# Fourth logits copied ahead of the tags; additions and statistics of batch b+2 woven into batch b's latents; expert weights loaded in halves

## The reference, cut to what matters

```python
x = x + attn_a(layernorm(x), w_in, w_out)          # 16 heads, causal
x = x + ffn(layernorm(x), gate_w, w1, b1, ...)     # L = 0
x = x + attn_b(layernorm(x), Wqa, Wqb, Wkva, ...)  # latents, rotary part, 16 heads
x = x + ffn(layernorm(x), gate_w, w1, b1, ...)     # L = 1, same weights

def ffn(x):
    logits = xf @ gate_w                      # 2048 x 8
    top_logits, top_idx = top_k(logits, 2)
    gates = softmax(top_logits)
    routed = sum over the two experts of gate * (gelu(xf @ w1[e] + b1[e]) @ w2[e] + b2[e])
    shared = gelu(xf @ shared_w1 + shared_b1) @ shared_w2 + shared_b2
    return routed + shared

q_latent = h @ Wqa                            # 512 -> 384
kv_comp = h @ Wkva                            # 512 -> 128 + 64, rotary on the 64
```

## Time and profile before

| | |
|---|---|
| median of three runs | 2495.82 us (2493.22 to 2500.20) |
| profiled execution, its own time | 2501.03 us |
| its span, first to last instruction | 2499.2 us |
| mean granted TensorE clock | 0.975 of full |
| TensorE busy | 94% |
| VectorE / ScalarE / GpSimd busy | 65% / 46% / 26% |

### The profile page before, as it was taken

The page is one execution under the profiler, slowest core; times in us unless marked ns, Lnnn a source line. Parts: engine busy times, 40 slices in busy tenths (PEclk is TensorE's granted clock), DMA queues, the critical chain, the costliest instruction groups (busy, mean ns, idle before and its releaser), DMA issues. The chain is left out here.

```text
span 2499.2 us, 41690 instructions
## 1 busy us (share of the span) xinstructions
PE 2359.7 (94%) x13140; PEld 2015.4 (81%) x13140; DVE 1630.5 (65%) x3774; ACT 1143.1 (46%) x2698; POOL 657.7 (26%) x546
## 2 busy tenths in 40 slices
PE   6999999999999999988998779999999999879997
PEld 5888888989898989767877568888888888657885
DVE  6555555555555555674545748988888888865446
ACT  4444444344444443442333336666666666532334
POOL 1111111111111010043221224444443434253223
PEclk9999999999999999989999989999999999899998
DMA  4424243333423335117664100000000000136765
GB/s 164 177 91 175 92 155 110 132 133 115 147 106 138 127 117 200 51 72 262 243 230 161 47 10 10 18 9 18 9 18 9 18 9 9 34 110 229 254 211 227
DMA packets 100852, 277.65 MB, mean 111 GB/s; under 512 B 8641, under 2 KB 9081, under 8 KB 95121
## 3 DMA queue, kind: packets, MB, share of 16 engines
q1 hardware_dynamic: 79888, 220.77, 24.9%
q0 software_dynamic: 11360, 37.76, 3.9%
q10 hardware_dynamic: 9504, 17.85, 2.3%
HBM read 131.34 MB, written 145.00 MB: 111 GB/s over the span
## 5 line engine op out<-in xcount | busy, mean ns | idle before, releaser
L609 DVE SCALAR_TENSOR_TENSOR x<-bank,inv,x 128x512 f32<-128x512 f32 x512 | 361.6, 744 | 173.2 <-PE bank L76 170.9
L619 DVE TENSOR_TENSOR hq_lo<-bank,hq_hi 128x512 fp32r<-128x512 f32 (+1 forms) x320 | 201.2, 637 | 272.6 <-ACT hq_hi L531 104.2
L74 PE MATMUL bank<-xT_hi,w_hi 128*128 128x512 f32 x864 | 351.2, 407 | 18.0 <-POOL w_lo L700 7.3
L497 ACT ACTIVATE s<-s,top 128x128 f32<-128x128 f32 (+3 forms) x512 | 282.1, 553 | 155.7 <-DVE top L601 155.7
L76 PE MATMUL bank<-xT_hi,w_lo 128*128 128x512 f32 x864 | 344.7, 399 | 0.0
L75 PE MATMUL bank<-xT_lo,w_hi 128*128 128x512 f32 x864 | 344.5, 399 | 0.0
L563 ACT ACTIVATE hq_hi<-bank 128x512 fp32r<-128x512 f32 x128 | 76.5, 597 | 388.2 <-PE bank L76 388.2
L74 PE MATMUL bank<-wo_hi,hq_hi 128*128 128x512 f32 (+1 forms) x576 | 233.6, 406 | 1.0 <-DVE xT_lo L178 0.7
L75 PE MATMUL bank<-wo_lo,hq_hi 128*128 128x512 f32 (+1 forms) x576 | 228.4, 396 | 0.3 <-issue 0.3
L76 PE MATMUL bank<-wo_hi,hq_lo 128*128 128x512 f32 (+1 forms) x576 | 227.8, 395 | 0.2 <-issue 0.2
L601 DVE CUSTOM_DVE_ANT_0 s<-bank,mask 128x128 f32<-128x128 f32 (+3 forms) x512 | 216.7, 479 | 4.3 <-PE bank L76 4.3
(11 more groups left out here) (285 smaller groups left out, 5859.3 us busy)
## 6 DMA issues: line engine op xcount, KB each, us to landing
sorted_x<-blank SPq DMA_DIRECT2D x48, 1584.0 KB, 10.9
arena<-split_w SPq DMA_DIRECT2D x16, 2048.0 KB
split_w<-arena SPq DMA_DIRECT2D x48, 512.0 KB, 3.0
raw<-dram_wr SPq DMA_DIRECT2D x24, 512.0 KB, 5.7
w_raw<-dram_wa SPq DMA_DIRECT2D x16, 512.0 KB, 3.7
arrived<-routed_y SPq DMA_DIRECT2D x8, 1024.0 KB, 7.9
row_pt_hi<-sorted_x ACTq DMA_DIRECT2D x22, 264.0 KB
row_pt_lo<-sorted_x ACTq DMA_DIRECT2D x20, 264.0 KB
```

What stands on the lines that cost most here:

```text
L74: nc.tensor.matmul(out, hi, mov_hi, start=first, stop=False)
L497: nc.scalar.activation(at, at, ACT.Exp, bias=m.top[:, b, t:t + 1], scale=-1.0, accum_out=m.rowsum[:, b, t:t + 1]).then_inc(a.probs_ready, 1)
L609: nc.vector.scalar_tensor_tensor(out=xt, in0=m.bank[6 + t % 2][:, :], scalar=m.inv[:, b, t:t + 1], in1=xt, op0=ALU.mult, op1=ALU.add).then ...
L619: return nc.vector.tensor_tensor(out, bank, hi.bitcast(F32), ALU.subtract).then_inc(done, 1)
```

## The change

In the gate, ScalarE's order of `tag(1)` and `logits(3)` is swapped, and TensorE waits for the chain's read before it turns the fourth logits into the same bank. Behind the tiles, scaling of batch 1 moves behind the transposes of batch 0 and that of batch 2 up into the FFN, that of batch 3 into latents 0; GpSimd's sum of batch 2 moves up too; the last `down` and its additions are split among the transposes of the next norm. In the latents, additions, statistics and start of a batch move one batch ahead: batch 1's stay at (0, OPEN); batch b + 2's additions stand behind tile 0, its statistics behind tile 1 of batch b, its start behind the subtractions. The up half of an expert's weights is loaded once its slot's last up product is done, the down half after the last down product, the bias after the last output.

```diff
-def latent_scalar(nc, act, m, l, rt, first, then):
+def latent_scalar(nc, act, m, l, rt, first, scale, then):
     for b in range(B):
         for i in range(OPEN, NT - 1):
...
         nc.scalar.activation(m.ctok[:, b, :], m.bank[7][:, :], ACT.Copy).then_inc(l.tok_out, 1)
         act.wait_ge(l.rope_added, b + 1)
         nc.scalar.activation(m.xT[HI][HALF:P, b, KQ, :], m.qf[HALF:P, :], ACT.Copy).then_inc(l.rope_hi, 1)
-
-
-def latent_vector(nc, dve, m, l, first):
+        if b == 0:
+            scale()
+
+
+def latent_vector(nc, dve, m, l, first, begin):
...
+        if b + 2 < B:
+            begin(b + 2)
         if b < B - 1:
             rotary(b)
 
...
 def latent_gpsimd(nc, pool, m, l, a, sum_up, then, combined):
     for b in range(B):
-        if b + 2 < B:
-            if b:
-                pool.wait_ge(l.rope_lo, b)
-            sum_up(b + 2)
+        if b == 1:
+            pool.wait_ge(l.rope_lo, b)
+            sum_up(B - 1)
         if b == B - 1:
             pool.wait_ge(l.rope_lo, b)
             then()
 
     def turn_logits(b):
         pe.wait_ge(g.lt_out, B * L + b + 1)
+        if b == 3:
+            pe.wait_ge(g.chain, CHAIN * (GROUPS * L + 1) + READ)
         for t in range(NT):
...
     for i in range(TILES):
         expert = pe.value_load(m.tab[0:1, E_AT + i:E_AT + i + 1], min_val=0, max_val=E - 1)
-        pe.wait_ge(rt.w_ready, 48 * expert + 48 * (E * L + 1))
+        pe.wait_ge(rt.w_ready, 64 * expert + 64 * (E * L + 1))
...
     down(B + 2, (0, 1, 2, 3))
-    tail(0)
-    down(B + 3, (0, 1, 2, 3))
+    down(B + 3, (0, 1))
+    tail(0, (0, 1))
+    down(B + 3, (2,))
+    tail(0, (2,))
+    down(B + 3, (3,))
+    tail(0, (3,))
...
     norm_tile(3, 3)
+    logits(3)
     tag(1)
-    logits(3)
...
     root(0)
-    for b in range(1, B if L else 2):
+    tail(0)
+    for b in range(1, B if L else 3):
         scale_scalar(nc, act, m, rt, g, L, b)
-    tail(0)
...
     add(B + 2)
-    tail(0)
+    tail(0, (0, 1))
+    if not L:
+        add(B + 3, (0, 1))
+        tail(0, (2,))
+        add(B + 3, (2,))
+        tail(0, (3,))
+        add(B + 3, (3,))
     if L:
         gather_vector(nc, dve, m, f, rt, L, 1)
         gather_vector(nc, dve, m, f, rt, L, 2)
-    add(B + 3)
-    if L:
+        add(B + 3)
         gather_vector(nc, dve, m, f, rt, L, 3)
...
-    for b in range(1, B if L else 2):
+    for b in range(1, B if L else 3):
         sum_gpsimd(nc, pool, m, rt, L, b)
...
+    def load_up(e):
+        s = e % 2
+        sp.dma_start(m.slots[:, s, 0:2048].bitcast(F32), ws[2 * e, :, :]).then_inc(rt.w_ready, 16)
+        sp.dma_start(m.slots[0:2, s, WCOLS:WCOLS + HF].bitcast(F32), bi[e, :, :]).then_inc(rt.w_ready, 16)
+
+    def load_down(e):
+        s = e % 2
+        sp.dma_start(m.slots[:, s, 2048:WCOLS].bitcast(F32), ws[2 * e + 1, :, :]).then_inc(rt.w_ready, 16)
+
+    def load_bias(e):
+        sp.dma_start(m.b2[:, e % 2, :], bs[e:e + 1, :].to_broadcast([P, D])).then_inc(rt.w_ready, 16)
...
     def load_slot(e):
-        s = e % 2
-        sp.dma_start(m.slots[:, s, 0:WCOLS].bitcast(F32).rearrange("p (a n) -> p a n", a=2),
-                     ws[2 * e:2 * e + 2, :, :].rearrange("a p n -> p a n")).then_inc(rt.w_ready, 16)
-        sp.dma_start(m.slots[0:2, s, WCOLS:WCOLS + HF].bitcast(F32), bi[e, :, :]).then_inc(rt.w_ready, 16)
-        sp.dma_start(m.b2[:, s, :], bs[e:e + 1, :].to_broadcast([P, D])).then_inc(rt.w_ready, 16)
+        load_up(e)
+        load_down(e)
+        load_bias(e)
...
     for e in range(2, E):
         end = sp.value_load(m.tab[0:1, END_AT + e - 2:END_AT + e - 1], min_val=1, max_val=TILES)
-        sp.wait_ge(rt.w_ready, 48 * (E * L + e))
+        sp.wait_ge(rt.w_ready, 64 * (E * L + e))
+        sp.wait_ge(rt.up_done, end + i0)
+        load_up(e)
+        sp.wait_ge(rt.y_done, end + i0)
+        load_down(e)
         sp.wait_ge(rt.y_out, end + i0)
-        load_slot(e)
+        load_bias(e)
...
+        def woven(collect, stats, start, tile):
+
+            def first(b, i):
+                if b == 0 and i == OPEN:
+                    collect(1)
+                    stats(1)
+                    start(1)
+                for (batch, t), place in later.items():
+                    if place == (b, i):
+                        tile(batch, t)
+                if b + 2 < B and i == 0:
+                    collect(b + 2)
+                if b + 2 < B and i == 1:
                     stats(b + 2)
             return first
...
-            def root_and_scale(b):
-                root(2)(b)
-                if b + 1 < B:
-                    scale_scalar(nc, act, m, rt, g, 0, b + 1)
-
-            latent_scalar(nc, act, m, lat, rt, woven(2, root_and_scale, nothing, tile(2)),
+            latent_scalar(nc, act, m, lat, rt, woven(nothing, root(2), nothing, tile(2)),
+                          lambda: scale_scalar(nc, act, m, rt, g, 0, B - 1),
                           lambda: [split_weights(nc, act, m, a2, True, 0, part, False) for part in range(3)])
...
-            def finished(b):
-                gather_vector(nc, dve, m, f, rt, 0, b)
-                stats(2)(b)
-
             ffn_vector(nc, dve, m, n, f, g, rt, a1, 0, stats(2), start(2), tiles(2))
-            latent_vector(nc, dve, m, lat, woven(2, finished, start(2), tile(2)))
+            latent_vector(nc, dve, m, lat, woven(lambda b: gather_vector(nc, dve, m, f, rt, 0, b), stats(2), start(2), tile(2)), start(2))
```

More of the change, by code:

```diff
@@ L1713, in ffn_sync @@
     if L:
-        sp.wait_ge(rt.w_ready, 48 * E)
+        sp.wait_ge(rt.w_ready, 64 * E)
     sp.wait_ge(rt.scattered[0], 32 * GT * (L + 1))
@@ L1723, in ffn_sync @@
         load_rows(sp, m, rt, xs_d, i, block)
-    sp.wait_ge(rt.w_ready, 48 * (E * L + 1))
+    sp.wait_ge(rt.w_ready, 64 * (E * L + 1))
     load_slot(1)
@@ L2091, in program, with woven_first @@
         later = {(b + 1, t): (b, t) for b in range(B - 1) for t in range(NT)}
-        def woven(r, stats, start, tile):
+        def woven_first(stats, start, tile):
             def first(b, i):
-                if r == 0:
-                    if b == 0 and i == OPEN:
-                        stats(1)
-                        start(1)
-                elif i == OPEN and b < B - 1:
-                    stats(b + 1)
-                    start(b + 1)
-                for (batch, t), place in (later if r else places).items():
+                if b == 0 and i == OPEN:
+                    stats(1)
+                    start(1)
+                for (batch, t), place in places.items():
                     if place == (b, i):
                         tile(batch, t)
-                        if t == NT - 1 and r == 0 and batch < B - 1:
+                        if t == NT - 1 and batch < B - 1:
                             start(batch + 1)
-                if r == 0 and (b, i) in ((0, 2), (1, OPEN)):
+                if (b, i) in ((0, 2), (1, OPEN)):
+                    stats(b + 2)
+            return first
+        def woven(collect, stats, start, tile):
+            def first(b, i):
+                if b == 0 and i == OPEN:
+                    collect(1)
+                    stats(1)
+                    start(1)
+                for (batch, t), place in later.items():
[4 more added lines that the diff above has]
+                if b + 2 < B and i == 1:
                     stats(b + 2)
@@ L2120, in tiles @@
             def tiles(r):
-                return lambda b: [tile(r)(b, t) for t in range(NT)]
+                return lambda b, ts=range(NT): [tile(r)(b, t) for t in ts]
             root(0)(0)
             tiles(0)(0)
-            attend_scalar(nc, act, m, a1, False, nothing, woven(0, root(0), nothing, tile(0)), root(1), tiles(1),
+            attend_scalar(nc, act, m, a1, False, nothing, woven_first(root(0), nothing, tile(0)), root(1), tiles(1),
                           prepare_scalar(nc, act, m, small_loaded))
             ffn_scalar(nc, act, m, n, f, g, rt, a1, 0, xs_d[0], root(2), tiles(2))
-            def root_and_scale(b):
-                root(2)(b)
-                if b + 1 < B:
-                    scale_scalar(nc, act, m, rt, g, 0, b + 1)
-            latent_scalar(nc, act, m, lat, rt, woven(2, root_and_scale, nothing, tile(2)),
+            latent_scalar(nc, act, m, lat, rt, woven(nothing, root(2), nothing, tile(2)),
+                          lambda: scale_scalar(nc, act, m, rt, g, 0, B - 1),
                           lambda: [split_weights(nc, act, m, a2, True, 0, part, False) for part in range(3)])
@@ L2161, in tiles, with after @@
             def tiles(r):
-                def after(b):
-                    for t in range(NT):
+                def after(b, ts=range(NT)):
+                    for t in ts:
                         tile(r)(b, t)
@@ L2169, in _ @@
             dve.wait_ge(m.const_set, CONSTS)
-            attend_vector(nc, dve, m, a1, False, woven(0, stats(0), start(0), tile(0)), both(1), tiles(1))
```

(14 more changed lines are left out.)

## The result

| | before | after |
|---|---|---|
| median of the runs shown together | 2497.35 us (8 runs, 2493.22 to 2504.29) | 2484.64 us (8 runs, 2480.9 to 2487.77) |
| ratio | 1 | 0.9945 [0.9932, 0.9959] |
| profiled execution, span | 2501.03, 2499.2 us | 2484.95, 2483.1 us |

13.7 us less by the ratio [10.2, 17.0], 16.1 by the spans of the two profiled executions. The forecast was 18.2 less, 2477.6 us; 2484.64 lies in its range of 2468 to 2489.

A forecast was written before the change was run, and what follows sets the result against it. It took TensorE, 94% busy, as the bound, improvable only where it waits or runs at half clock. Terms 0 - 8.0 + 2.3 + 0 - 4.2 - 8.3 = -18.2 took the median 2495.8 to 2477.6 us, range 2468 to 2489.

The forecast's parts named there:

- Logits, 0: Gate: copying the fourth logits ahead of tag 1 gains 0, since the product's signal is late, not the order.
- Halves, -8.0: Expert tiles, both FFNs: loading weights in halves removes four waits, 6.8 us, and half clock behind two, 1.2 us.
- one of its signs of being wrong: Tile loop: more TensorE waits for VectorE's hidden part would show the prediction wrong.
- Tail, +2.3: End of first FFN: splitting the last down projection and scaling batch 1 later costs 2.3 us, bounds -3 and +4.
- two tiles to 1368.4: Tail: TensorE starts the last down projection at 1364.4 after 3.1 us idle and ends two tiles at 1368.4.
- Batch 0, 0: Latents, batch 0: additions and statistics of batch 2 fit into VectorE's idle 7.8 us, costing 0.
- Batch 1, -4.2: Latents, batch 1: with batch 3's additions and statistics inside it takes 23.4 us instead of 27.63.
- Batch 2, -8.3: Latents, batch 2: without additions or statistics it takes 19.1 us against 27.44, 1.5 of it for half clock.
- Signal: Rival, gate: the late signal of the fourth logits does go with the order, a further -13 us, 2464.6; chance 0.06.
- Latents little: Rival, latents: ScalarE's order and contention hold copies back, leaving -1.1 us there, 2486.7 in all; chance 0.12.
- Halves nothing: Rival, expert tiles: traffic is the limit, so halves give nothing, -10.2 us in all, 2485.6; chance 0.11.
- Slower by the stores: Rival, tile loop: earlier half loads slow output stores, 0.3 us in each of 78 tiles, 23 us, 2509; chance 0.05.

The follow-up runs named there:

- e12: The kernel before with only the logits' order changed, the fourth logits copied ahead of tag 1: 2506.9 us, ratio 1.0004 to before.
- e2: The changed kernel with GpSimd pausing its scatters, in both FFNs, until the fourth logits are copied: 2496.2 us, ratio 0.9993 to before.
- e9: The changed kernel with the tail's order and batch 1's scaling put back as before the change: 2487.8 us, ratio 0.9932 to before.
- e8: The changed kernel with an expert's weights again loaded whole behind its last output: 2489.6 us, ratio 0.9960 to before.
- e4: The changed kernel with batch 3's scaling in two ScalarE gaps of batch 0, sum 3 ahead of batch 0's rotary sum: 2479.9 us, ratio 0.9920 to before.
- e10: As e6, but GpSimd holds sums 2 until the Newton steps of batch 1's statistics are over: 2482.4 us, ratio 0.9913 to before.
- e11: As e10, but with the tail in the order before the change: 2485.1 us, ratio 0.9922 to before.
- e6: e4 plus batch 1's scaling ahead of the tail, sums 2 and 3 held until batch 1's and 2's additions: 2477.7 us, ratio 0.9912 to before.
- e1: The kernel before with only the expert weights loaded in halves: 2494.6 us, ratio 0.9985 to before.

## Why the prediction was nearly right

The sum was -18.2; the tiles, the tail and the latents gave -13.5 in the profile, the ratio -13.7. That these two agree is partly luck: the gate's +1.7, the start's -0.5 and attention b's -3.8 lie between the former and the 16.1 of the spans. The median is 7.0 us above the forecast: 4.7 are the terms, the other 2.3 the base (2495.82 of three runs, 2497.35 of eight) and the spread.

*Logits, 0: right*, and for the reason given: the signal, not the order (e12, e2).

*Halves, -8.0: -6.3, by the times about -4.* All waits for weights went, as the row said. Failed: "all four waits go: 6.8 us ... 1.2 more" was taken as a sum with nothing on the other side. TensorE's waits for VectorE's hidden part grew by 2.1 us in this pair of profiles, by 1.5 in the mean of all. The term had to be taken net, between its bounds. The half clock was worth a little more than the 1.2: the products' busy time in the loops fell by 1.8 us. The prediction also read the earlier trace rows as all the waits for VectorE there are, "2.0 us in four"; these are the first FFN's, and the second had 0.9 us in two more. More of these waits was one of its signs of being wrong, and it came (eleven against six).

*Tail, +2.3: +5.0* (e9: 4.6 by the stretch, 3.2 by the times), outside its bound of +4. This is the mis-sized term. Its main step was exact: additions beside the sums at 1.69 us each. Failed: "two tiles to 1368.4", 4.0 us for 12 products; behind the idle time of 3.48 us they took 5.25 (1363.12 to 1368.37), at the 1.2 GHz level. In e8's profile the clock did not fall, 2.84 us for the same twelve (1362.62 to 1365.46), and that stretch is 41.6 us. The transposes behind the twelve, in after and in e8, and the first product in e8:
```profile
1368.37 1.21 PE L200 MATMUL bank<-ident,xn 128*128 128x128 f32 x8
...
1362.62 0.47 PE L74 MATMUL bank<-w2b_hi,hq_hi 128*128 128x512 f32 x1 [3.38 <-DVE x L1483]
...
1365.46 1.03 PE L200 MATMUL bank<-ident,xn 128*128 128x128 f32 x8
```
The rest: the wait 0.3 longer, later steps slower by as little each, variance 0.6 longer beside the sums. Counted from D, the first transposes came at 29.2 us, forecast 26.6; e8 has 26.5.

*Batch 0, 0: right.* 14.1 us from its first transpose to batch 1's first product, 13.9 before, with additions and statistics of batch 2 inside. In the profiles of e4, e8, e10 and e11 it was 15.0, so the 0 may be 1 us short.

*Batch 1, -4.2: -4.6*, 23.0 us where 23.4 were forecast, with the wait for ScalarE's copy that the prediction named (3.35 us). e4 shows its cause right: without the scaling in front the batch is 17.9.

*Batch 2, -8.3: -7.6*, 19.8 us for 19.1: at half clock longer behind batch 1's last wait. Its products were busy for 18.2 us, against 16.2 in e4 and e6, where the clock stayed up; 1.5 us had been forecast for that.

*Rivals.* Signal: no (e12). Latents little: no. Halves nothing: no (e1, e8), though by the times only about half of the term came, with a wide interval. Slower by the stores: no; something like it costs 1.5 to 2.1 us, not 23. The time lies 1 us from that of "halves give nothing", 2485.6, but not by its cause: it is reached by the tail and half of the halves' term together.

## What to carry to other kernels

Work moved off a critical wait lands somewhere: look on its new place for what stands behind it in order (ScalarE's scaling before copies) and for the other engine that it now runs beside (VectorE's two-input additions beside GpSimd's sums), and put it where its own engine has a gap, as e4 did. A saved wait is worth its length less what the next wait grows by. Before shortening a wait at a gate, ask what will then run without a break: here 24 scatters in a row, which held TensorE up for about three times as long as the wait had taken.

## What the runs showed of the hardware

- From 12 us into a run of scatters issued back to back by GpSimd (1.27 us each) TensorE's signals come late, the fourth logits' by 6.4 to 11 us in the first FFN and 10.5 to 10.8 in the second, to about the end of the run. With a pause of 3.1 us in the run the same signal was in time (e2). In the 24 that followed it in a row TensorE was held up from the 15th us on, to a product each 2.1 us, at a DMA share of 1.0 first and of 0.5 to 0.65 later. What is shared was not found.
- Nearly the same idle time is followed by half clock for no, a short or a long time: twelve products behind 3.4, 3.3 and 3.5 us took 2.84, 4.20 and 5.25 us (e8, e4 and after). This moves the profile by 2 us in the tail alone.
- Beside GpSimd's sums (1.27 us each) VectorE's two-input additions go from 0.62 to 1.69 us, the row statistics of the norm (2.47 us for four tiles) not at all.
